# Steps in another order on four engines of a two-layer attention and expert kernel, and a drain of GpSimd moved

## What is computed

```
x = x + tanh(g_xattn[0]) * L0_xattn(ctx_512, layernorm(x))   # two graph attention layers, adjacency = layernorm(x)
x = x + tanh(g_ffn[0])   * L0_ffn(layernorm(x))              # ternary weights: down(silu(gate(x)) * up(x)), 704 inner
x = x + tanh(g_xattn[1]) * L1_xattn(ctx_512, layernorm(x))   # top 76 of 256 scores per row, mixed with layernorm(x)
x = x + tanh(g_ffn[1])   * L1_ffn(layernorm(x))              # 8 experts, each token through its best 2
```

## Time and profile before

| | us |
|---|---|
| median of 3 executions | 216.94 (216.5 to 217.57) |
| the profiled execution | 217.63 |
| its span in the profile | 215.9 |

### The profile page before, as it was taken

The page is one execution under the profiler, slowest core; times in us unless marked ns, Lnnn a source line. Parts: engine busy times, 40 slices in busy tenths (PEclk is TensorE's granted clock), DMA queues, the critical chain, the costliest instruction groups (busy, mean ns, idle before and its releaser), DMA issues.

```text
span 215.9 us, 3840 instructions
## 1 busy us (share of the span) xinstructions
PE 203.1 (94%) x1286; PEld 159.3 (74%) x1286; DVE 136.5 (63%) x469; ACT 85.1 (39%) x187; POOL 86.1 (40%) x107
## 2 busy tenths in 40 slices
PE   8999979999999998999989999999999999999980
PEld 7787854435786446878978998999994479999960
DVE  3596897999997978997797488663415621211130
ACT  2678661998200547032524336122234342222100
POOL 8175316620001120036460324545587844622442
PEclk9999999999999999999999999999999999999995
DMA  6758318119999114917144222223242300022224
GB/s 185 178 200 254 120 40 265 54 55 372 415 419 418 74 49 156 376 30 245 35 120 147 24 29 24 47 41 47 27 89 47 73 12 5 8 29 24 25 23 45
DMA packets 16795, 26.06 MB, mean 121 GB/s; under 512 B 4105, under 2 KB 12421, under 8 KB 16774
## 3 DMA queue, kind: packets, MB, share of 16 engines
q1 hardware_dynamic: 11328, 20.14, 26.0%
q0 software_dynamic: 4064, 5.24, 13.9%
q10 hardware_dynamic: 1382, 0.41, 0.9%
HBM read 21.34 MB, written 5.51 MB: 124 GB/s over the span
## 4 chain that ended last, share of the span: by engine, by line
PE 45%; DVE 29%; issue 7%; ACT 7%; DMA 6%; POOL 3%; DVEq 1%; POOLq 0%; ACTq 0%
PE PS L2128 19%; PE PS L2160 9%; DMA out_dram<-a,ids_late 5%; PE PS L1831 4%; PE PS L2180 3%; DVE stat L1083 3%; DVE hT L1475 3%; PE PS L2193 2%; ACT a L854 2%; PE PS L1895 2%; DVE work L1161 2%; PE PS L2114 2%; DVE x L1335 2%; DVE mv L1090 1%; DVE work L1147 1%
## 5 line engine op out<-in xcount | busy, mean ns | idle before, releaser
L2128 PE MATMUL PS<-hT,e 128*128 128x128 f32 x512 | 62.0, 276 | 1.1 <-ACT hT L983 1.1
L2128 PEld LDWEIGHTS PS<-hT,e 128*128 128x128 f32 x512 | 60.1, 192 | 2.8 <-ACT hT L983 1.9
L2013 PE MATMUL PS<-xnT,e 128*128 128x512 f32 x88 | 39.6, 598 | 1.9 <-DVE hT L1475 1.1
L2013 PEld LDWEIGHTS PS<-xnT,e 128*128 128x128 f32 x88 | 16.1, 190 | 22.1 <-issue 17.4
L1731 DVE TENSOR_TENSOR hT<-th,PS 128x512 f32<-128x512 f32 x15 | 10.3, 686 | 34.2 <-PE PS L2128 33.9
L2160 PE MATMUL PS<-e,hT 128*128 128x256 f32 x128 | 30.5, 381 | 0.2 <-DVE x L1513 0.2
L2160 PEld LDWEIGHTS PS<-e,hT 128*128 128x128 f32 x128 | 23.2, 190 | 2.9 <-issue 0.3
L656 POOL TENSOR_TENSOR rstd<-veps,nhalf 128x2 f32<-128x2 f32 x12 | 8.7, 728 | 39.4 <-DVE veps L1092 39.3
L722 POOL DMA_INDIRECT out_dram<-a,ids_early x8 | 13.0, 1626 | 24.2 <-ACT a L1017 11.4
L2027 PE MATMUL PS<-e,hT 128*128 128x256 f32 x96 | 21.7, 383 | 0.0
L993 ACT ACTIVATE th<-PS 128x512 f32<-128x512 f32 x16 | 9.5, 593 | 26.9 <-PE PS L2128 23.5
(11 more groups left out here) (314 smaller groups left out, 323.0 us busy)
## 6 DMA issues: line engine op xcount, KB each, us to landing
e<-e_in SPq DMA_DIRECT2D x24, 512.0 KB, 8.0
x<-x_in SPq DMA_DIRECT2D x2, 512.0 KB, 6.2
graph_rows<-e SPq DMA_DIRECT2D x4, 256.0 KB, 2.1
out_dram<-x SPq DMA_DIRECT2D x4, 256.0 KB, 2.5
xn_rows<-xn SPq DMA_DIRECT2D x4, 256.0 KB, 2.4
e<-gw_in SPq DMA_DIRECT2D x1, 768.0 KB
e<-uw_in SPq DMA_DIRECT2D x1, 640.0 KB
e<-dw_in SPq DMA_DIRECT2D x1, 640.0 KB
```

What stands on the lines that cost most here:

```text
L2013: mm = pe.matmul(PS[:, bank, :], w[:, k, it * P:(it + 1) * P], xnT[:, h, k, :], start=(k == 0), stop=(k == 1))
L2128: mm = pe.matmul(PS[:, bank + q, f * P:(f + 1) * P], w[:, k * F + f * P:k * F + (f + 1) * P], xgT[x_at][:, k, :], start=(k == 0), stop=(k ...
```

## The change

Entries of the four lists change places; nothing is computed that wasn't before.

- PE: `list(0)` stands three products of `ffn_down` later, and `turn_x(0)` ahead of the last two products of `ffn_down` and of `lost(1)`. `turn_x(3)` and `up3(2)` stand ahead of `turn_moe` of pairs 2 and 3, `up1(3)` ahead of the late half's router. `turn_x(4)` and `up3(3)` stand ahead of `down(1)`, and `up1(4)` ahead of `down(2)`.
- ACT: the silu of `ffn_up(1, 3)` ahead of `norm_moe` of pairs 0 and 1; `copy_x(1)` ahead of `attn_scale(2)`; `copy_x(3)` between the two `norm_moe` of the late half; the copies of `turn_moe` 2 and 3 behind `silu(2)`; `scale_y` of blocks 0 to 2 later; `odds(1)`, with its two table loads, behind `copy_x(5)`.
- DVE: `gate(1)` ahead of `norm_moe(3)` (L1526), with `spare` and `shares` (small router arithmetic) behind that; the search step that `FILL` put behind `norm_moe(1)` stands behind the feed-forward gate of `ffn_up(1, 3)`, where one was already; the four last steps of the early search behind the addition of `ffn_down` of pair 2 (L1484), not ahead of it.
- POOL: the drain moves from between `gather_over(1)` and `scatter(6)` to the list's end, behind `gather(15)` and ahead of the over-loop.

```diff
-                    ("router", 0), ("router", 1), ("ffn_down", 2, 0), ("count", 0), ("ffn_down", 2, 1), ("list", 0),
-                    ("ffn_down", 3, 0), ("ffn_down", 3, 1), ("lost", 1),
-                    ("turn_x", 0), ("up1", 0), ("turn_x", 1), ("up3", 0),
+                    ("router", 0), ("router", 1), ("ffn_down", 2, 0), ("count", 0), ("ffn_down", 2, 1), ("ffn_down", 3, 0, 0, 3),
+                    ("list", 0), ("ffn_down", 3, 0, 3), ("ffn_down", 3, 1, 0, 4), ("turn_x", 0), ("ffn_down", 3, 1, 4), ("lost", 1),
+                    ("up1", 0), ("turn_x", 1), ("up3", 0),
...
-            FILL = {("move", 2, 1): 1, ("ffn_up", 0, 5): 10, ("attn_scale", 0): 1, ("norm_moe", 1): 1, ("ffn_up", 1, 3): 1, ("ffn_up", 1, 4): 2, ("tokens", 0): 2, ("ranks", 0): 1, ("odds", 0): 4}
+            FILL = {("move", 2, 1): 1, ("ffn_up", 0, 5): 10, ("attn_scale", 0): 1, ("ffn_up", 1, 3): 2, ("ffn_up", 1, 4): 2, ("tokens", 0): 2, ("ranks", 0): 1, ("ffn_down", 2): 4}
...
-                      ("scatter", 5), ("gather_over", 0), ("gather_over", 1), ("retire",), ("scatter", 6), ("gather", 10), ("gather", 11), ("scatter", 7),
+                      ("scatter", 5), ("gather_over", 0), ("gather_over", 1), ("scatter", 6), ("gather", 10), ("gather", 11), ("scatter", 7),
                       ("gather", 12), ("gather", 13), ("scatter", 8), ("gather_over", 2), ("gather_over", 3), ("scatter", 9),
-                      ("gather", 14), ("gather", 15)]
+                      ("gather", 14), ("gather", 15), ("retire",)]
```

More of the change, by code:

```diff
@@ L430, in build @@
                     ("kept", 0), ("ffn_up", 1, 2), ("ffn_up", 1, 3), ("ffn_up", 1, 4), ("turn_moe", 0), ("turn_moe", 1), ("ffn_up", 1, 5),
-                    ("router", 0), ("router", 1), ("ffn_down", 2, 0), ("count", 0), ("ffn_down", 2, 1), ("list", 0),
-                    ("ffn_down", 3, 0), ("ffn_down", 3, 1), ("lost", 1),
-                    ("turn_x", 0), ("up1", 0), ("turn_x", 1), ("up3", 0),
+                    ("router", 0), ("router", 1), ("ffn_down", 2, 0), ("count", 0), ("ffn_down", 2, 1), ("ffn_down", 3, 0, 0, 3),
+                    ("list", 0), ("ffn_down", 3, 0, 3), ("ffn_down", 3, 1, 0, 4), ("turn_x", 0), ("ffn_down", 3, 1, 4), ("lost", 1),
+                    ("up1", 0), ("turn_x", 1), ("up3", 0),
                     ("up1", 1), ("kept", 1), ("turn_x", 2), ("up3", 1), ("down", 0),
-                    ("up1", 2), ("turn_moe", 2), ("turn_x", 3), ("turn_moe", 3), ("up3", 2), ("router", 2), ("list", 1), ("router", 3), ("up1", 3), ("down", 1),
-                    ("turn_x", 4), ("up3", 3), ("count", 1), ("down", 2),
-                    ("up1", 4), ("turn_x", 5), ("up3", 4), ("down", 3),
+                    ("up1", 2), ("turn_x", 3), ("up3", 2), ("turn_moe", 2), ("turn_moe", 3), ("up1", 3), ("router", 2), ("list", 1), ("router", 3),
+                    ("turn_x", 4), ("up3", 3), ("down", 1), ("count", 1),
+                    ("up1", 4), ("down", 2), ("turn_x", 5), ("up3", 4), ("down", 3),
                     ("up1", 5), ("turn_x", 6), ("up3", 5), ("list", 2), ("down", 4),
@@ L446, in build @@
                      ("ffn_up", 1, 0), ("attn_scale", 0), ("ffn_up", 1, 1), ("attn_scale", 1), ("ffn_up", 1, 2),
-                     ("norm_moe", 0), ("norm_moe", 1), ("ffn_up", 1, 3), ("ffn_up", 1, 4),
+                     ("ffn_up", 1, 3), ("norm_moe", 0), ("norm_moe", 1), ("ffn_up", 1, 4),
                      ("turn_moe", 0), ("turn_moe", 1), ("ffn_up", 1, 5), ("odds", 0),
-                     ("copy_x", 0), ("attn_scale", 2), ("silu", 0), ("copy_x", 1), ("attn_scale", 3), ("silu", 1), ("copy_x", 2),
-                     ("norm_moe", 2), ("norm_moe", 3), ("turn_moe", 2), ("silu", 2), ("copy_x", 3), ("turn_moe", 3), ("scale_y", 0),
-                     ("silu", 3), ("scale_y", 1), ("copy_x", 4), ("scale_y", 2), ("silu", 4), ("odds", 1), ("copy_x", 5), ("scale_y", 3),
+                     ("copy_x", 0), ("copy_x", 1), ("attn_scale", 2), ("silu", 0), ("attn_scale", 3), ("silu", 1), ("copy_x", 2),
+                     ("norm_moe", 2), ("copy_x", 3), ("norm_moe", 3), ("silu", 2), ("turn_moe", 2), ("turn_moe", 3),
+                     ("silu", 3), ("copy_x", 4), ("scale_y", 0), ("scale_y", 1), ("silu", 4), ("scale_y", 2), ("copy_x", 5), ("odds", 1), ("scale_y", 3),
                      ("silu", 5), ("copy_x", 6), ("scale_y", 4), ("silu", 6), ("copy_x", 7), ("scale_y", 5)]
@@ L468, in build @@
                      ("attn_scale", 3), ("gate", 0), ("attn", 1), ("attn_out", 2), ("moe_stats", 2),
-                     ("attn_out", 3), ("moe_stats", 3), ("norm_moe", 2), ("spare", 0), ("norm_moe", 3), ("shares", 0), ("gate", 1),
+                     ("attn_out", 3), ("moe_stats", 3), ("norm_moe", 2), ("gate", 1), ("norm_moe", 3), ("spare", 0), ("shares", 0),
                      ("choices", 2), ("coefs", 0), ("choices", 3), ("gate", 2),
```

## The result

The changed kernel takes 216.34 us (median of 19 runs, lowest 214.01, two runs far above all others left out of the ratio) against 217.42 us for the kernel before (median of 19). The ratio is 0.9938, with a 95% interval of 0.9921 to 0.9956: 1.35 us faster, between 0.96 and 1.72. The forecast was 1.55 us. For the median itself it was 215.4, 0.9 under what was measured; half of that is the kernel before, 217.42 here and 216.94 when the forecast was made. The profiled execution of the changed kernel has a span of 215.1 us, 0.8 under the span before.

A forecast was written before the change was run, and what follows sets the result against it. PE was taken to bound up to about 175 us, then POOL's scatter chain. PE's 3.45 gained less 1.9 at the drain gives 1.55 us faster: median 215.4, own range 214.4 to 216.4, wider range 213.3 to 217.0.

The forecast's parts named there:

- 3.45 us of PE: Sum of PE's closed pauses less new ones, gained by up1(5) and held to the over-loop: 3.45 us.
- 1.9 us given back at the drain: Drain between gather(15) and the over-loop delays the first scatter from 175.56 to 177.4: 1.9 us lost, bounds 0 to 2.6.
- down(0) waits for x from DVE: PE at down(0): 0.3 us idle after, 0.57 with its pause, so -0.1; another us lost if DVE gained only 0.97.
- the gains at list and up1(0): PE ahead of block 0: ffn_down products cover both waits, gaining 0.77 us at list and 0.74 at up1(0).
- I leave 0.5 + 0.27 = 0.77: PE at turn_moe 2 and 3: of 1.54 us, 0.77 stays because the second still waits for its norm_moe; 0.77 goes.
- The term at up1(5): PE at up1(5): copy now ahead of two table loads, so the wait of 0.37 and its 0.27 go: 0.64 us gained.
- turn_x(0): PE at turn_x(0): new pause of 0.6 us for gather 0, taking 2.6 from issue to landing; costs 0.87.
- The drain's own terms: POOL ahead of the over-loop: drain outlives gather(15)'s issue by 2.65, register and loop 1.1, copies 1.44, then 0.9 to the scatter.
- the free drain: Rival, POOL at the over-loop: drain ends with gather(15)'s issue and costs nothing; 213.5 us, chance 0.15.
- another spacing in it: Sign of being wrong, over-loop: the chain of scatters has another spacing than before; no size given.
- The long drain: Rival, POOL at the over-loop: drain lasts all its 5.97 us, scatter starts at 180.75; 218.7 us, chance 0.07.
- the late gather: Rival, PE at turn_x(0): gather 0 takes 3.7 us, not 2.6, so PE waits 1.1 more; 216.5 us, chance 0.14.

The follow-up runs named there:

- Drain back: Changed kernel with the drain in its old place, between gather_over(1) and scatter(6): 214.41 us, ratio 0.9869 to the kernel before.
- drain only: Kernel before with only the drain moved, to the end of POOL's list ahead of the over-loop: 219.25 us, ratio 1.0099.
- First gaps back: Drain back, with PE's list(0), turn_x(0) and last ffn_down products in the order of the kernel before: 213.86 us, ratio 0.9846.
- no drain: Drain back without its drain, so none in POOL's list: 214.44 us, ratio 0.9892 to the kernel before.
- the second: Second profile, of the changed kernel run once more with nothing altered: 216.14 us, ratio 0.9947 to the kernel before.
- two drains: Changed kernel with a second drain at the old place, ahead of scatter(6): 217.35 us, ratio 0.9997 to the kernel before.

## Why the prediction was right, point by point

**The two large terms held.** The forecast was 3.45 us of PE and 1.9 us given back at the drain. Measured at zb, PE gave 93.30 - 89.90 = 3.40. The drain took 93.02 - 91.32 = 1.70 on the changed kernel, and 1.68 on the one before. Drain back and drain only, which split the change in two, show it with their times as well: 2.8 faster, 2.15 slower. The mechanism was right: a gain that PE carries to zb, and a part of it lost at the drain. That each term came out within 0.2 us is luck in part, since errors inside each cancelled, as the next points show.

**Two terms of PE's sum were wrong, and cancelled by luck.** Up to down(0) the terms come to 2.04 us; measured are 27.65 - 26.23 = 1.42. The step that failed is "down(0) waits for x from DVE. PE is some 2 us sooner there, and so are DVE's steps". DVE's steps were not: DVE sets the pace at down(0), and what PE gained beyond DVE's own gain went into the wait at kept(1) and turn_x(0). First gaps back shows it: without the gains at list and up1(0) nothing is lost. The prediction named this possibility, and kept a us for it in the range. From down(0) to zb the terms come to 1.41 and measured are 3.40 - 1.42 = 1.98. The step there is "I leave 0.5 + 0.27 = 0.77": the second turn_moe doesn't wait at all in the changed kernel, so 1.54 went and not 0.77. The term at up1(5) was right to 0.1.

**turn_x(0)** waits 1.03 us and not 0.6. Gather 0 was issued at 93.68, and PE went on at 96.61: 2.9 us, where the prediction had 2.6. What it took too small is the time from the gather's last packet of rows to PE's start, an estimate of 0.25 that came from no row: here the packets ran to 96.0, and it is 0.6. By the Trainium skill, "DMA: Bandwidth & Descriptors", section "Anatomy of one DMA — SWDGE (gpsimd) path", the estimate was 2.3, which is farther off. The longer wait cost nothing, since DVE sets the pace behind it.

**The drain's own terms** were off, and right together by luck. It outlived the last issue by 171.36 - 167.96 = 3.4 us, not 2.65. That the upper end of the range, 3.3 from the final drain, is closer is no more than luck: what sets the length is how many indirect DMAs the drain has behind it (last section), 38 here, 26 at the old place and 24 at the end. Register and loop took 172.50 - 171.36 = 1.1, as taken. The copies took 0.42, not 1.44; in the earlier trace rows they ran behind a gather. That the old place had cost nothing held: with no drain the first scatter starts where it does with the drain back, 91.32 after turn_moe(0). The 12 ns of the Trainium skill, "VectorE: DVE Perf Modes", section "The DRAIN you can't avoid", are stated for the boilerplate's drains. The drain at the loop is the kernel's own call and took 6857 ns, so that sentence was no ground for the free drain.

**What was missed** is behind the first scatter. The prediction took that chain as rigid, and named another spacing in it as a sign of being wrong; that sign came, in one gap. In the changed kernel it is 210.64 - 173.93 = 36.71 long, before 210.79 - 175.56 = 35.23, since block 12's scatter lands late. And the end behind the last scatter is shorter, 4.5 and not 5.1, because the final drain has less to do (below). The sum over the first profile: -3.40 + 1.72 + 1.48 - 0.60 + 0.05 for the start = -0.75, where the rounded spans differ by 0.8. Over the second it is -1.25 without the start, close to the timed 1.15 to 1.35.

**The rivals.** The changed kernel did not reach the 213.5 of the free drain. The drain back comes near to it with 214.41, but there the drain stands at its old place. The long drain and the late gather did not come: the first scatter stands at 173.93, not at 177.3, and gather 0 took 2.9 us and not 3.7, its delay hidden by DVE.

## What to carry to other kernels

Closing a gap of the busiest engine pays only up to the next place where that engine waits for another: find that wait first, and count what the other engine gains. A drain, or any wait, that is moved on an engine that seems half idle has its price where that engine enters the chain that ends last. Count there also what the sequencer used to do early, beside other work, and now does behind the wait. And undo parts of a good change one by one: here one line of it, the drain's new place, cost more than half of what the rest had won.

## What the runs showed of the hardware

A drain of GpSimd costs more the more indirect DMAs were issued since the one before it. In the eleven traces a drain ended 0.9 us after the last packet of an indirect DMA with 12 issued since the drain before, 1.4 with 24 or 26, 1.9 with 38, and 2.4 with 50: some 0.04 us for each. It is their number and not the time that counts, for 12 gave 0.9 both at the loop of two drains, 16 us after the drain before, and at the end of the changed kernel, 38 us after it. This shows behind the last scatter too. The span ends 4.5 to 4.6 us after the last scatter's issue where a drain stood at the loop (12 DMAs since, changed, drain only, two drains), 5.0 to 5.1 where it stood in the middle (24 since), and 6.1 to 6.2 with none in the list. The final drains agree: in the kernel with no drain,

```profile
L70 POOLq DRAIN  x1: 5786/5786/5786, 207.6 to 207.6; - x1
```

it lasts to 213.4, 5.9 us beyond the last scatter's issue at 207.50; with the drain back the whole span ends 5.1 us after its last scatter's issue, at 212.7. So by the profiles a drain in the middle, where no last chain waits behind it, takes a us off the end. The times of these two kernels, with ratios of 0.9869 and 0.9892, overlap and don't show it.

A fetch of instructions (0.02 MB) that met a scatter's packets went with a landing 0.7 to 1.8 us late, in five profiles of five, and in none of the six where it came behind them. That the fetch is the cause is argued from this alone. A change that moves one engine's queue against another's by a us or two can run into one, or out of it.
